# Cross attention on one core: key and value units taken by turns, the keys made two quads in front of their scores

## The chip, the core and the metric

The kernel runs on one core of a Trainium2 chip. Time is the device time of one execution in microseconds (us), less is better. Three runs of the kernel before took 2381.77, 2382.19 and 2385.43 us; their median is 2382.19 us.

The engines are called PE (TensorE, matmuls), DVE (VectorE), ACT (ScalarE), POOL (GpSimd) and SP (SyncE, which issues most transfers). PEld is PE's weight load, which overlaps the matmuls. Each engine takes its instructions in the order in which they are written; between engines, semaphores say who may go on.

## The reference, cut to what matters

A decoder layer of three parts, each with a residual and a layer norm: causal self attention, cross attention to a context of 722 positions, and a gated feed forward. The change is in the cross attention and in the passage from it to the feed forward.

```python
q = (query @ Wq.T + bq).reshape(b, lq, HEADS, HEAD_DIM)
k = (key @ Wk.T + bk).reshape(b, lk, HEADS, HEAD_DIM)
v = (value @ Wv.T + bv).reshape(b, lk, HEADS, HEAD_DIM)
scores = jnp.einsum('bqhd,bkhd->bhqk', q * scale, k)
probs = jax.nn.softmax(scores, axis=-1)
attn = jnp.einsum('bhqk,bkhd->bqhd', probs, v).reshape(b, lq, HIDDEN)
return attn @ Wo.T + bo
```

There are 32 batches of 100 query tokens, 512 features and 16 heads of 32. Key and value both come from the same context, `ctx_1024` (32 x 722 x 512). Everything is fp32; the large products are made of three products of a high and a low part each.

## The kernel before

**Quads, pairs and steps.** The cross attention works in steps. Two steps, a pair, serve one quad: four heads of one batch. A batch has four quads, all batches have 128, so there are 256 steps (`STEPS`). The scores of quad q are written at step 2q; its weighted sum (probabilities times values) is written four steps, two pairs, later (`SUM_AFTER`).

**Units.** The keys of a batch are made in 8 key units: unit u gives one half of the 722 positions (384 or 338 columns, `HALVES`) for one quad, so a quad needs two. The values of a batch are made in 6 value units of 128 positions and 512 columns each; in 7 of 32 batches there are 5, because their last rows share a unit with other batches (tails). Each unit is 12 matmuls of PE (line 69). The tables `KEYS_AHEAD`, `V_STEP` and `FOURTH_V_STEP` give each unit its step: before, the two key units of a quad stand in the pair just in front of the pair of its scores. A pair holds two key units and one or two value units.

**The order on PE.** In a pair: the scores (L2057, 36 matmuls, into the four-bank tile `ps_s`), the units of the pair (`units_of_pair`, sorted: all keys, then all values), and the weighted sum of the quad two pairs back (`weighted_sum`, L2081).

**Two banks.** Units and weighted sums take the two PSUM banks `ps_p` in strict turn. `wait_bank` makes PE wait, before it writes the n-th item, until the (n-2)th has been read out: a key unit by DVE (`k_low`), a value unit by ACT (`v_done`), a weighted sum by DVE (`scaled`).

**ACT.** For a pair: four exponentials (`exps`, L1687; each reads one head of the scores and needs DVE's maxima), the key units' high parts (`take_keys`, L1667), the value units (`take_values`, L1675) and four transfers of the diagonal blocks of the turned probabilities (`move_diagonal`, L1697).

**DVE.** For a pair: the result of a weighted sum out of PSUM (`take_result`, L1847), four maxima (L1820), four block transposes of the exponentials (`turn_blocks`, L1829), the low parts of two key units (`low_keys`, L1872), a reciprocal (L1835) and its transpose (L1840).

**POOL and SP.** POOL splits each batch's context into high and low parts, four pieces, in the pairs that begin at steps 6 and 10 of the batch two before (L1554, L1556), and spreads the inverses. SP issues twelve transfers of turned blocks per quad, the context and the queries.

**The start.** Four steps (from -4) lie ahead of the first scores. DVE takes no key unit before it has read a maximum over all partitions, which POOL makes (L1865).

**The end.** The last pairs are written out by hand: the first five output projections (`project_o`, into `ps_y`), the last two score quads, the last weighted sums, the sum and norm of the first tiles (`second_sum`, `normalise`), the transposes (`transpose_x2`). `TAIL` is the first quad whose weighted sum takes bank 0 whatever its turn. `project_o(0, 0)` waits for the split output weights (`wo_low`, DVE L1973), the split first outputs (`o_low`, DVE L1978 and POOL), all keys and values, and the results of all quads below `TAIL`.

Of the kernel before, what the change touches and what calls it, by code (L numbers as in the profile page):

```python
# [1 line left out]

# [11 lines left out]
KD = D // P  # L14
# [7 lines left out]
QUADS = H // 4  # L22
# [1019 lines left out]
def phase_cross_and_feed_forward(nc, sem, passed, ctxT, cq_d, held, bk, bv, o_d, x1_d, wo, bo, w_gate, w_up, w_down, biggest, out):  # L1042
# [19 lines left out]
    KEYS_AHEAD = 2  # L1062
# [21 lines left out]
    TAIL = MAIN // 2 - 1  # L1084
# [6 lines left out]
    with ExitStack() as ctx:  # L1091
# [159 lines left out]
        units_of_pair = {s: sorted(unit_at.get(s, []) + unit_at.get(s + 1, [])) for s in every_step if s % 2 == 0}  # L1251
# [97 lines left out]
        with nc.Block() as block:  # L1349
# [312 lines left out]
            def _(act):  # L1662
# [41 lines left out]
                def take_units(kind, s):  # L1704
                    for which, b, n in unit_at.get(s, []):
                        if which == kind:
                            (take_keys if kind == "k" else take_values)(b, n)

                def quad_at(s):
                    if s >= 0:  # L1710
                        exps(2 * s)
                    take_units("k", s)
                    if s >= 0:
                        exps(2 * s + 1)
                    take_units("k", s + 1)
                    if s >= 0:
                        exps(2 * s + 2)
                        exps(2 * s + 3)
                    if s > 1:
                        move_diagonal(s // 2 - 1)  # L1720
                    take_units("v", s)
                    take_units("v", s + 1)
# [93 lines left out]
            def _(dve):  # L1816
# [63 lines left out]
                def quad_at(s, first_sum=None):  # L1880
# [4 lines left out]
                    low_keys(s)  # L1885
                    turn_blocks(s, 0)
                    low_keys(s + 1)
                    turn_blocks(s, 1)
                    if s == MAIN:
                        take_result(sum_at[s])  # L1890
                    invert(s // 2)
                    turn_blocks(s + 1, 0)
                    turn_inverses(s // 2)
                    if first_sum is not None:
                        second_sum(0, first_sum)
                    turn_blocks(s + 1, 1)
# [92 lines left out]
                quad_at(MAIN, first_sum=0)  # L1989
# [16 lines left out]
                take_biased(QUADS * B - 2)  # L2006
                normalise("a", 3, x2[:, 3, :])
                low_x2(0, 1)
                low_x2(0, 2)
                second_sum(0, 4)  # L2010
# [9 lines left out]
            def _(pe):  # L2020
                def keys_unit(b, u):
                    m, (first, end) = u // 2, HALVES[u % 2]
                    wait_bank(pe, "k", b, u)
# [4 lines left out]
                def values_unit(b, i):  # L2028
                    rows = P if i < ST - 1 else LAST
                    if i == 0:  # L2030
                        pe.wait_ge(c_low, KD * (b + 1))
# [82 lines left out]
                def feed_forward(w, view):  # L2114
# [53 lines left out]
                    weighted_sum(last - 1)  # L2168
                    transpose_x2(0, 1)
                    project_o(0, 4)  # L2170
                    transpose_x2(0, 2)
# [86 lines left out]
```

## Time and profile before

| what | us |
|---|---|
| median of three runs | 2382.19 |
| the profiled execution, whole | 2380.97 |
| its span (first to last instruction) | 2379.2 |
| first scores of the cross attention | at 506.97 |
| scores of quad 125 (the 126th) | at 1838.84 |
| scores of quad 126 | at 1851.26 |
| first gate matmul of the feed forward | at 1889.89 |

Times of the trace are counted from the span's start. The rows below are of five kinds: windows (busy time of each engine in a stretch), the waits of an engine added up, and the timelines of PE, of ACT, POOL and DVE in one pair, the one whose scores start at 1242.84.

### The profile page before, as it was taken

The page shows a single profiled execution, that of the slowest core. Times are in us where ns is not written, and L with a number is a line of the kernel's source. Part 1 is how long each engine was busy: PE and PEld are TensorE (multiplying, and loading weights), DVE is VectorE, ACT ScalarE, POOL GpSimd, SP SyncE. Part 2 cuts the span into 40 slices and gives each one's busy share as a digit, 9 for nine tenths or more (in the row PEclk, how much of TensorE's full clock was granted, in tenths as well). Part 3 has the DMA queues.
Part 4 walks back from the last instruction along what each step waited for, and adds up shares of the span by engine and source line. Part 5 has one row for each costly group of instructions (what it writes and reads, how often), then busy time and mean ns, then how long its engine had stood idle before and what let it go on. Part 6 is the DMA issues. An engine that isn't in the chain of part 4 may idle for free.

```text
span 2379.2 us, 61357 instructions
## 1 busy us (share of the span) xinstructions
PE 2322.6 (98%) x23178; PEld 2039.2 (86%) x23178; DVE 1642.2 (69%) x2566; ACT 1139.5 (48%) x3066; POOL 1016.0 (43%) x1337
## 2 busy tenths in 40 slices
PE   8999979999999999999999999999999899999999
PEld 7878858978888888888888888888888799998998
DVE  4666788847878788787778787787787734435342
ACT  5878852234555555455554555555555442231321
POOL 4767677334334344334343344343332333333332
PEclk9999989999999999999999999999999999999999
DMA  7444478547777777777777777777777741102010
GB/s 191 130 130 114 121 210 322 208 118 188 196 197 197 199 196 202 196 199 201 194 194 203 191 203 197 195 203 189 197 199 209 214 133 36 50 18 66 8 33 23
DMA packets 256370, 384.77 MB, mean 162 GB/s; under 512 B 118296, under 2 KB 133720, under 8 KB 256088
## 3 DMA queue, kind: packets, MB, share of 16 engines
q1 hardware_dynamic: 231512, 330.66, 49.9%
q10 hardware_dynamic: 24576, 50.36, 7.8%
q8 instruction: 176, 2.88, 0.5%
q14 instruction: 106, 0.87, 0.1%
HBM read 126.33 MB, written 40.60 MB: 70 GB/s over the span
## 4 chain that ended last, share of the span: by engine, by line
PE 76%; DVE 1%; issue 1%; DMA 0%; ACT 0%; POOL 0%; ACTq 0%; POOLq 0%; DVEq 0%
PE D_ps_p L69 43%; PE D_ps_s L2057 7%; PE D_ps_p L2081 6%; PE E_ps_u L69 6%; PE E_ps_g L69 6%; PE E_ps_d L69 5%; PE E_ps_y L69 3%; PE E_ps_t L2110 0%; DVE D_columns L1820 0%; DMA D_pT<-D_turned 0%; DVE D_turned L1829 0%; DVE E_wo_low L1973 0%; ACT D_e L1687 0%; DVE D_keys L1872 0%; ACTq L1697 0%
## 5 line engine op out<-in xcount | busy, mean ns | idle before, releaser
L1687 ACT ACTIVATE D_e<-D_ps_s,D_columns 128x726 f32<-128x726 f32 x512 | 441.4, 868 | 442.3 <-DVE D_columns L1820 442.3
L1820 DVE TENSOR_REDUCE D_columns<-D_ps_s 128x1 f32<-128x726 f32 x512 | 432.3, 907 | 121.6 <-PE D_ps_s L2057 121.6
L1829 DVE STREAM_TRANSPOSE D_turned<-D_e 128x768 f32<-128x768 f32 x512 | 491.2, 960 | 0.0
L69 PE MATMUL D_ps_p<-D_ctx_high,cross_wk_high 128*128 128x384 f32 (+1 forms) x1024 | 345.6, 338 | 0.0
L69 PE MATMUL D_ps_p<-D_ctx_high,cross_wk_low 128*128 128x384 f32 (+1 forms) x1024 | 332.7, 325 | 0.0
L69 PE MATMUL D_ps_p<-D_ctx_low,cross_wk_high 128*128 128x384 f32 (+1 forms) x1024 | 332.3, 325 | 0.0
L69 PE MATMUL D_ps_p<-cross_wv_high,D_ctx_high 128*128 128x512 f32 (+1 forms) x656 | 269.6, 411 | 5.6 <-DVE D_keys L1872 4.1
L1538 POOL COPY D_turned<-D_turned_inv 128x100 f32<-128x100 f32 x128 | 34.8, 272 | 551.2 <-DVE D_turned_inv L1840 551.2
L69 PE MATMUL D_ps_p<-cross_wv_high,D_ctx_low 128*128 128x512 f32 (+1 forms) x656 | 257.3, 392 | 0.0
L69 PE MATMUL D_ps_p<-cross_wv_low,D_ctx_high 128*128 128x512 f32 (+1 forms) x656 | 257.1, 392 | 0.0
L1675 ACT ACTIVATE D_values<-D_ps_p 128x512 f32<-128x512 f32 (+1 forms) x185 | 110.8, 599 | 242.4 <-PE D_ps_p L69 210.9
L1556 POOL TENSOR_TENSOR D_ctx_low<-D_craw,D_ctx_high 128x722 fp32r<-128x722 f32 x124 | 217.1, 1751 | 10.0
L69 PEld LDWEIGHTS D_ps_p<-D_ctx_high,cross_wk_high 128*128 128x128 f32 x1024 | 192.0, 188 | 15.5
L650 ACT ACTIVATE A_e<-A_e,A_neg_max 100x100 f32<-100x100 f32 x512 | 186.4, 367 | 37.1 <-DVE A_neg_max L779 36.3
L1953 DVE SCALAR_TENSOR_TENSOR E_gated<-E_ps_u,E_gated 128x320 f32<-128x320 f32 x120 | 59.0, 491 | 209.6 <-ACT E_gated L1756 209.6
L69 PEld LDWEIGHTS D_ps_p<-D_ctx_low,cross_wk_high 128*128 128x128 f32 x1024 | 192.3, 188 | 0.0
L69 PEld LDWEIGHTS D_ps_p<-D_ctx_high,cross_wk_low 128*128 128x128 f32 x1024 | 192.2, 188 | 0.0
L1599 POOL TENSOR_TENSOR E_hidden_low<-E_gated,E_hidden_high 128x320 fp32r<-128x320 f32 x120 | 105.0, 876 | 182.6 <-ACT E_hidden_high L1749 182.6
L2081 PEld LDWEIGHTS D_ps_p<-D_pT,D_values 128*32 128x32 f32 x5920 | 126.9, 108 | 47.9 <-issue 46.0
L1533 POOL TENSOR_SCALAR D_o<-D_o,D_columns 128x100 f32<-128x100 f32 x125 | 66.9, 535 | 235.8 <-DVE D_o L1847 235.8
L69 PEld LDWEIGHTS D_ps_p<-cross_wv_high,D_ctx_high 128*128 128x128 f32 (+1 forms) x656 | 122.8, 187 | 50.8 <-DVE D_keys L1872 16.8
L2081 PE MATMUL D_ps_p<-D_pT,D_values 128*32 128x100 f32 x5920 | 155.8, 250 | 2.7 <-DVE D_keys L1872 1.7
(271 smaller groups left out, 5594.7 us busy)
## 6 DMA issues: line engine op xcount, KB each, us to landing
D_pT<-D_turned SPq DMA_DIRECT2D x1536, 96.0 KB, 2.5
D_pT<-D_turned ACTq DMA_DIRECT2D x512, 96.0 KB, 2.8
D_craw<-in_ctxT SPq DMA_DIRECT2D x124, 361.0 KB, 3.9
self_v<-wstage SPq DMA_DIRECT2D x25, 256.0 KB, 2.6
A_v<-self_v SPq DMA_DIRECT2D x32, 200.0 KB
self_o<-A_o SPq DMA_DIRECT2D x32, 200.0 KB, 4.0
x<-C_x SPq DMA_DIRECT2D x5, 1280.0 KB, 6.0
cross_q<-C_qo SPq DMA_DIRECT2D x20, 320.0 KB, 4.2
```

The costliest lines, as they stand in the source:

```text
L69: last = pe.matmul(out, lhs(a, k), rhs(b, k), start=(k == 0 and n == 0), stop=(k == chunks - 1 and n == len(terms) - 1))
L650: act.activation(head, head, ACT.Exp, bias=neg_max[:, b % 2, h:h + 1], accum_out=rowsum[:, half, i:i + 1]).then_inc(exp_done, 1)
L1533: pool.tensor_scalar(rows, rows, bv_c[:, m:m + 1], None, ALU.add).then_inc(o_done, 1)
L1556: pool.tensor_tensor(cs[b % 2][1][:, k, 0:S], craw[k % 2][:, :], cs[b % 2][0][:, k, 0:S].bitcast(F32), ALU.subtract).then_inc(c_low, 1)
L1599: pool.tensor_tensor(hs[1][:, c, cols], gated[u % 2][:, :], hs[0][:, c, cols].bitcast(F32), ALU.subtract).then_inc(hl_done, 1)
L1675: act.activation(vs[b % 2][0:rows, i, :], bank("v", b, i)[0:rows, 0:D], ACT.Copy).then_inc(v_done, 1)
L1687: act.activation(e[n // 2 % 2][:, n % 2, 0:PARTS * PART].rearrange("p (a c) -> p a c", a=PARTS), parts_of(n), ACT.Exp, bias=neg_max[:, n % ...
L1820: dve.tensor_reduce(neg_max[:, n % 4:n % 4 + 1], parts_of(n), AX.XY, ALU.max, negate=True)\
L1829: dve.transpose(turned[quad % 2][:, :, 2 * (s % 2) + h, :].rearrange("p j (t r) -> p t j r", r=32), e[s % 2][:, h, :].rearrange("p (t j r) ...
L1953: dve.scalar_tensor_tensor(gated[u % 2][:, :], ps_u[u % 2][:, 0:HALF], FSCALE, gated[u % 2][:, :], ALU.mult, ALU.mult).then_inc(h_done, 1)
L2057: last = pe.matmul(of_head[:, j, a, 0:end - first], qs[q][rows, quad % 2, :, :].rearrange("p a q -> p (a q)"), ks[k][rows, quad % 2, first ...
L2081: last = pe.matmul(out[HD * j:HD * (j + 1), 0:T], values[:, c:c + HD], pT[quad % 2][:, :, j, 32 * i:32 * i + QB], start=(i == 0), stop=(i ...
```

## The change

Six edits, in the code below:

1. `KEYS_AHEAD` goes from 2 to 4: the key units of a quad stand two pairs in front of its scores, no longer one. The last pairs have fewer units, the first ones more.
2. In a pair PE takes key and value units by turns (`by_turns`): key, value, key, and the second value if there is one; then the weighted sum. PE's wait for the split context (`c_low`) goes from the first value unit of a batch to its first key unit, which now stands in the same pair.
3. ACT: first key unit after the first exponential as before; then the three other exponentials, the first value unit, the second key unit, the diagonal transfers, the second value unit.
4. DVE: the low part of the second key unit goes from between the first two transposes to the very end of the pair.
5. `TAIL` is one less. PE's last pair is written by hand: scores, projection 0, weighted sum, projection 1.
6. At the end, the first sum of the second norm stands in front of the transposes of its pair; the weighted sum of quad 126 and its result go behind projection 4.

```diff
-    KEYS_AHEAD = 2
+    KEYS_AHEAD = 4
...
-    TAIL = MAIN // 2 - 1
+    TAIL = MAIN // 2 - 2
...
-        units_of_pair = {s: sorted(unit_at.get(s, []) + unit_at.get(s + 1, [])) for s in every_step if s % 2 == 0}
+        def units_in(s, which):
+
+            return [u for u in unit_at.get(s, []) + unit_at.get(s + 1, []) if u[0] == which]
+
+        def by_turns(s):
+
+            both = itertools.zip_longest(units_in(s, "k"), units_in(s, "v"))
+            return [u for pair in both for u in pair if u is not None]
+
+        units_of_pair = {s: by_turns(s) for s in every_step if s % 2 == 0}
...
                     if s >= 0:
                         exps(2 * s)
-                    take_units("k", s)
+                    take(keys[:1])
                     if s >= 0:
                         exps(2 * s + 1)
-                    take_units("k", s + 1)
-                    if s >= 0:
                         exps(2 * s + 2)
                         exps(2 * s + 3)
+                    take(values[:1])
+                    take(keys[1:])
                     if s > 1:
                         move_diagonal(s // 2 - 1)
-                    take_units("v", s)
-                    take_units("v", s + 1)
+                    take(values[1:])
...
                     low_keys(s)
+                    if s == MAIN:
+                        second_sum(0, 0)
                     turn_blocks(s, 0)
-                    low_keys(s + 1)
                     turn_blocks(s, 1)
                     if s == MAIN:
                         take_result(sum_at[s])
+                    turn_blocks(s + 1, 0)
                     invert(s // 2)
-                    turn_blocks(s + 1, 0)
+                    turn_blocks(s + 1, 1)
                     turn_inverses(s // 2)
-                    if first_sum is not None:
-                        second_sum(0, first_sum)
-                    turn_blocks(s + 1, 1)
+                    low_keys(s + 1)
...
                 second_sum(0, 3)
-                take_biased(QUADS * B - 2)
                 normalise("a", 3, x2[:, 3, :])
                 low_x2(0, 1)
+                second_sum(0, 4)
+                take_biased(QUADS * B - 2)
                 low_x2(0, 2)
-                second_sum(0, 4)
...
                 def keys_unit(b, u):
                     m, (first, end) = u // 2, HALVES[u % 2]
+                    if u == 0:
+                        pe.wait_ge(c_low, KD * (b + 1))
                     wait_bank(pe, "k", b, u)
...
-                    if i == 0:
-                        pe.wait_ge(c_low, KD * (b + 1))
...
                     project_o(0, 3)
-                    weighted_sum(last - 1)
                     transpose_x2(0, 1)
                     project_o(0, 4)
+                    weighted_sum(last - 1)
...
-                for s in range(FIRST, MAIN + 1):
-                    if 0 <= s < STEPS and s % 2 == 0:
+                for s in range(FIRST, MAIN, 2):
+                    if s >= 0:
                         scores(s // 2)
...
+                scores(last - 1)
                 project_o(0, 0)
+                weighted_sum(last - 3)
                 project_o(0, 1)
```

**PE, one pair with a single value unit in the middle of the cross attention.** Each unit is shown by its first matmul (11 more follow). `cross_wk` marks a key unit, `cross_wv` a value unit, `D_ps_p0` and `D_ps_p1` are the two banks, `D_ps_s` the scores, the row with `D_pT` the weighted sum. Before:

```order
7007 L2057 MATMUL D_ps_s<-D_keys_7891,D_queries_low_7895 128x238 x4
7008 L69 MATMUL D_ps_p1<-D_ctx1_high_7882,cross_wk_high 128x384
...
7020 L69 MATMUL D_ps_p0<-D_ctx1_high_7882,cross_wk_high 128x338
...
7032 L69 MATMUL D_ps_p1<-cross_wv_high,D_ctx1_high_7882 128x512
...
7044 L2081 MATMUL D_ps_p0<-D_pT1_7903,D_values0_7896 32x100 x24
```

Of the change:

```order
7031 L2067 MATMUL D_ps_s<-D_keys_7891,D_queries_low_7895 128x238 x4
7032 L70 MATMUL D_ps_p1<-D_ctx1_high_7882,cross_wk_high 128x384
...
7044 L70 MATMUL D_ps_p0<-cross_wv_high,D_ctx1_high_7882 128x512
...
7056 L70 MATMUL D_ps_p1<-D_ctx1_high_7882,cross_wk_high 128x338
...
7068 L2091 MATMUL D_ps_p0<-D_pT1_7903,D_values0_7896 32x100 x24
```

The value unit now stands between the two key units. The bank of the first key unit is asked for again by the second key unit and not by the value unit; the weighted sum asks for the bank of the value unit and not for that of the second key unit.

**ACT, one pair with a single value unit.** `D_e` rows are exponentials, `D_keys` and `D_values` rows read a unit out. Before:

```order
896 L1687 ACTIVATE D_e0_7897,D_columns_7906<-D_ps_s,D_columns_7906 128x726
897 L1667 ACTIVATE D_keys_7891<-D_ps_p0,D_columns_7906 128x384
898 L1687 ACTIVATE D_e0_7897,D_columns_7906<-D_ps_s,D_columns_7906 128x726
899 L1667 ACTIVATE D_keys_7891<-D_ps_p1,D_columns_7906 128x338
900 L1687 ACTIVATE D_e1_7898,D_columns_7906<-D_ps_s,D_columns_7906 128x726 x2
901 L1697 DMA D_pT0_7902<-D_turned0_7899 32x768 x4
902 L1675 ACTIVATE D_values1_7901<-D_ps_p0 128x512
```

Of the change:

```order
898 L1698 ACTIVATE D_e0_7897,D_columns_7906<-D_ps_s,D_columns_7906 128x726
899 L1678 ACTIVATE D_keys_7891<-D_ps_p0,D_columns_7906 128x384
900 L1698 ACTIVATE D_e0_7897,D_columns_7906<-D_ps_s,D_columns_7906 128x726
901 L1698 ACTIVATE D_e1_7898,D_columns_7906<-D_ps_s,D_columns_7906 128x726 x2
902 L1686 ACTIVATE D_values1_7901<-D_ps_p1 128x512
903 L1678 ACTIVATE D_keys_7891<-D_ps_p0,D_columns_7906 128x338
904 L1708 DMA D_pT0_7902<-D_turned0_7899 32x768 x4
```

The value unit goes in front of the second key unit and of the transfers, and stays behind all four exponentials.

**DVE, one pair in the middle, of the change.** Before, the row with 128x338 stood between the two transposes of `D_e0`.

```order
1538 L1857 TENSOR_TENSOR D_o1_7905<-D_ps_p1,D_pT1_7903 128x100
1539 L1830 TENSOR_REDUCE D_columns_7906<-D_ps_s 128x1 x4
1540 L1882 SCALAR_TENSOR_TENSOR D_keys_7891<-D_ps_p0,D_columns_7906,D_keys_7891 128x384
1541 L1839 STREAM_TRANSPOSE D_turned0_7899<-D_e0_7897 128x6x4x32 x2
1542 L1839 STREAM_TRANSPOSE D_turned0_7899<-D_e1_7898 128x6x4x32
1543 L1845 RECIPROCAL D_columns_7906<-D_columns_7906 128x4
1544 L1839 STREAM_TRANSPOSE D_turned0_7899<-D_e1_7898 128x6x4x32
1545 L1850 STREAM_TRANSPOSE D_turned_inv_7893<-D_columns_7906 128x128
1546 L1882 SCALAR_TENSOR_TENSOR D_keys_7891<-D_ps_p0,D_columns_7906,D_keys_7891 128x338
```

The low part of the second key unit is the last row of the pair now.

## Rows read from the trace of the kernel before

**Rows 1.** Windows: bounds, length, busy (instructions) of PE, PEld, DVE, ACT, POOL, clock, DMA.

```profile
499.70:507.00 7.30, 7.29 (x28) 5.59 (x28) 0.43 (x1) 0.60 (x1) 0.92 (x2) 0.77 0.00 0
506.97:1838.84 1331.87, 1331.87 (x15565) 1151.43 (x15564) 1056.00 (x1622) 686.74 (x1456) 524.13 (x801) 1.00 0.74 197
...
1860.91:1889.89 28.98, 22.97 (x208) 17.40 (x209) 22.52 (x41) 8.64 (x14) 5.80 (x9) 0.88 0.94 280
```

**Rows 2.** Waits of PE's weight loads, 500 to 1870: us, times, longest.

```profile
PEld D_ps_p L69 <- DVE D_keys L1872: 12.4, 74, 0.4
```

**Rows 3.** Timeline of PE in one pair: start, us, engine, line, operation.

```profile
1242.84 0.50 PE L2057 MATMUL D_ps_s<-D_keys,D_queries_high 32*128 32x242 f32 x8
...
1244.09 0.44 PE L69 MATMUL D_ps_p<-D_ctx_high,cross_wk_high 128*128 128x384 f32 x1
...
1246.28 0.31 PE L69 MATMUL D_ps_p<-D_ctx_high,cross_wk_high 128*128 128x338 f32 x1
...
1247.81 0.31 PE L69 MATMUL D_ps_p<-D_ctx_low,cross_wk_high 128*128 128x338 f32 x1
1247.97 0.32 PE L69 MATMUL D_ps_p<-D_ctx_high,cross_wk_low 128*128 128x338 f32 x1
1248.17 0.50 PE L69 MATMUL D_ps_p<-cross_wv_high,D_ctx_high 128*128 128x512 f32 x1
1248.51 0.39 PE L69 MATMUL D_ps_p<-cross_wv_low,D_ctx_high 128*128 128x512 f32 x1
...
1251.12 1.26 PE L2081 MATMUL D_ps_p<-D_pT,D_values 128*32 128x100 f32 x48
1252.30 0.50 PE L2057 MATMUL D_ps_s<-D_keys,D_queries_high 32*128 32x242 f32 x8
```

**Rows 4.** Timeline of PE at the start, from a value unit into a key unit.

```profile
491.31 0.39 PE L69 MATMUL D_ps_p<-cross_wv_high,D_ctx_low 128*128 128x512 f32 x1
491.54 0.33 PE L69 MATMUL D_ps_p<-D_ctx_high,cross_wk_high 128*128 128x384 f32 x1
```

**Rows 5.** Timeline of ACT in the same pair.

```profile
1245.98 0.87 ACT L1687 ACTIVATE D_e<-D_ps_s,D_columns 128x726 f32<-128x726 f32 x1 [3.62 <-DVE D_columns L1820]
...
1246.84 0.57 ACT L1667 ACTIVATE D_keys<-D_ps_p,D_columns 128x384 fp32r<-128x384 f32 x1
1247.30 0.87 ACT L1687 ACTIVATE D_e<-D_ps_s,D_columns 128x726 f32<-128x726 f32 x1
...
1251.22 0.60 ACT L1675 ACTIVATE D_values<-D_ps_p 128x512 f32<-128x512 f32 x1 [0.67 <-PE D_ps_p L69]
```

**Rows 6.** Timelines of DVE and POOL in the same pair.

```profile
1244.21 3.38 DVE L1820 TENSOR_REDUCE D_columns<-D_ps_s 128x1 f32<-128x726 f32 x4 [0.98 <-PE D_ps_s L2057]
1247.50 0.61 DVE L1872 SCALAR_TENSOR_TENSOR D_keys<-D_ps_p,D_columns,D_keys 128x384 fp32r<-128x384 f32 x1
1248.03 0.97 DVE L1829 STREAM_TRANSPOSE D_turned<-D_e 128x768 f32<-128x768 f32 x1
1248.92 0.55 DVE L1872 SCALAR_TENSOR_TENSOR D_keys<-D_ps_p,D_columns,D_keys 128x338 fp32r<-128x338 f32 x1
...
1252.62 0.22 DVE L1847 TENSOR_TENSOR D_o<-D_ps_p,D_pT 128x100 f32<-128x100 f32 x1
...
1247.93 1.75 POOL L1556 TENSOR_TENSOR D_ctx_low<-D_craw,D_ctx_high 128x722 fp32r<-128x722 f32 x1
```

**Rows 7.** Timelines of DVE and PE around the stall at the start.

```profile
499.04 1.08 DVE L1872 SCALAR_TENSOR_TENSOR D_keys<-D_ps_p,D_columns,D_keys 128x384 fp32r<-128x384 f32 x2
...
499.71 0.55 PE L69 MATMUL D_ps_p<-cross_wv_high,D_ctx_high 128*128 128x512 f32 x1 [4.06 <-DVE D_keys L1872]
```

**Rows 8.** Timelines of DVE and PE in the last pairs.

```profile
1848.71 3.60 DVE L1973 TENSOR_TENSOR E_wo_low<-E_wo_raw,E_wo_high 128x512 fp32r<-128x512 f32 x2
1852.23 2.18 DVE L1978 TENSOR_TENSOR E_acts_low<-E_acts_raw,E_acts_high 128x640 fp32r<-128x640 f32 x1
...
1858.54 1.24 PE L2081 MATMUL D_ps_p<-D_pT,D_values 128*32 128x100 f32 x48 [1.73 <-DVE D_keys L1872]
```

More of the change, by code:

```diff
@@ L1 @@
 from contextlib import ExitStack
+import itertools
 import math
@@ L1703, in _, with take @@
                 act.wait_ge(b_loaded, 32)
[L1704 to L1707, printed above, removed]
+                def take(units):
+                    for kind, b, n in units:
+                        (take_keys if kind == "k" else take_values)(b, n)
                 def quad_at(s):
+                    keys, values = units_in(s, "k"), units_in(s, "v")
                     if s >= 0:
                         exps(2 * s)
-                    take_units("k", s)
+                    take(keys[:1])
                     if s >= 0:
                         exps(2 * s + 1)
-                    take_units("k", s + 1)
-                    if s >= 0:
                         exps(2 * s + 2)
                         exps(2 * s + 3)
+                    take(values[:1])
+                    take(keys[1:])
                     if s > 1:
                         move_diagonal(s // 2 - 1)
-                    take_units("v", s)
-                    take_units("v", s + 1)
+                    take(values[1:])
                 def high_o(g):
@@ L1878, in maxima, with quad_at @@
                     maximum(2 * s + 1)
-                def quad_at(s, first_sum=None):
+                def quad_at(s):
                     if s - 2 in sum_at:
@@ L1988, in _ @@
                 last_first_low()
-                quad_at(MAIN, first_sum=0)
+                quad_at(MAIN)
                 normalise("a", 0, x2[:, 0, :])
```

## The prediction

> **What bounds the kernel now.** I read the windows first, then the waits, then one pair of the cross attention on every engine. From the first scores to those of quad 125, 1331.87 of the 2379 us of the span, PE is busy all the time at full clock; DVE is busy 79% and ACT 52% of it [rows 1]. So PE sets the pace and only what PE itself loses counts. Nearly nothing shows as idle, since matmuls overlap; the loss has to be read as the distance between starts. Inside a key unit of 338 columns matmuls follow at 0.153 to 0.16 us, and a value unit's at 0.23 (its last one to the next unit, too) [rows 3, 4]. From the last key matmul to the first value matmul it is 0.20, and from that to the second 0.34 [rows 3]. The sum of both excesses, 0.05 and 0.11, is 0.16 us per pair. Its cause is in the waits: PE's weight load there waits for DVE's `D_keys`, 12.4 us in 74 times, 0.17 each [rows 2]. The value unit takes the bank of the first key unit, whose low part DVE ends only at 1248.11, 0.06 before the value unit starts [rows 3, 6]: DVE must first make four maxima of the scores written just before.
>
> **The pair, part by part.** I count from the start of the scores, 1242.84. Before: first key unit +1.25, second +3.44, value unit +5.33, weighted sum +8.28, next scores +9.46 [rows 3]. There are 125 pairs from quad 0 to quad 125, of which 70 hold one value unit and 55 two (from the step tables).
>
> By turns, the order is key, value, key, (value), sum. Who waits for whom now:
> - Value unit at +3.44. It wants the bank of the sum or value before it, which is read early; the wait is gone. It takes 12 x 0.228 = 2.73, to +6.17.
> - Second key unit at +6.17. It wants the bank of the first, whose low part ends at +5.27 [rows 6]. ACT and DVE treat the first key unit as before. Slack 0.9. It takes 12 x 0.153 = 1.84, to +8.01.
> - Second value unit, or the weighted sum, at +8.01. It wants the first value unit's bank, read by ACT behind all four exponentials. ACT: exponential at +3.14, key at +4.00, exponential at +4.46 [rows 5]; from one exponential to what follows it is 0.86, so the others start at +5.32 and +6.18 (the maxima are there at +4.66 [rows 6]), and the value is read from +7.04 to +7.64, its 0.60 as now [rows 5]. PE asks for it with the weight load, 0.15 ahead of +8.01. Slack 0.2 in front of a value unit, near 0.45 in front of the sum, whose weights don't load ahead. This is the tightest place of the change.
> - The sum behind a second value unit wants the second key unit's bank, at +10.7. DVE's low part of it now ends the pair. DVE as a whole does the same work: the result of the sum came at +9.78 [rows 6], so the low part ends by then. The same holds for a pair with one value unit, in which the next first key unit wants that bank, at +10.5. Slack 0.7.
> - The next pair's scores need keys that were made a pair earlier, and their four exponentials, ended by +7.1. No wait. DVE ends at +10.0 and the next maxima can start at 9.30 + 1.37 = +10.67: DVE still idles 0.6 per pair and doesn't become the bound.
> - ACT's diagonal transfers move behind the second key unit's readout, by 2 us; they are for a sum a whole pair later (+17). Queued behind them on ACT is only the second value unit, which PE ends at about +10.9. SP's transfers start when the last transpose is done, which is earlier than now, as the low part has left the space ahead of it.
> - PE's wait for the split context moves from the value unit to the first key unit of the same pair. POOL ends the last piece at 1249.68 [rows 6], and the key unit that would need it starts at 1252.30 + 1.25 = 1253.55. Nothing waits. Moving a wait that is satisfied costs nothing.
>
> So a pair loses its 0.16: 125 x 0.16 = 20.0 us by the one pair, 125 x 0.17 = 21.3 by the waits. I take **-21**. Bounds: what the four edges do when all waits are satisfied isn't in the trace for key into value; value into key is, at 0.23 with nothing added [rows 4], and that is the nearest row. At worst that spacing is intrinsic, and the gain 0; at best the pairs with longer waits (the longest are 0.4 [rows 2]) bring it to -24.
>
> The Trainium skill would have the spacing smaller (TensorE: Matmul & The Clock Gate, Back-to-back issue gap: columns over 2.4 GHz plus 2.5 ns), that is 0.216 us for 512 columns and 0.143 for 338. By that estimate PE would be back at the value's bank at about +7.75 and not +8.01, near enough to wait for ACT in the pairs with two value units. The trace has 0.23 and 0.153 [rows 3, 4], and the measurement decides.
>
> **The start.** PE has two banks. Before, value, key, key went ahead of the stall; the fourth item waited until 499.71 for DVE, which takes keys only from 499.04 [rows 7]. Now the third item (the second key unit) wants the first key unit's bank and stalls to the same 499.7, with 1.84 us of work less behind it. After the stall come key 1.84, key 2.08 (12 x 0.174 from [rows 3]), value, key, value: 11.3 us, to 511.0 at full clock. The clock row gives 0.77 of full clock for the 7.3 us after the stall [rows 1], a loss of 7.3 x 0.23 = 1.7 us; with the same loss the first scores start at 512.7, against 506.97. That is **+5.8**, of which 3.9 are the two key units that move here from the end. PE now idles 6 us instead of 4, so the low stretch could start sooner and cost less, or last longer: +4.1 with no loss, +7.5 with twice the loss.
>
> An idle array is throttled and regains its clock after work, says the Trainium skill (TensorE: Matmul & The Clock Gate, What's actually happening); the 0.77 behind a stall of 4.06 us agrees.
>
> **The end.** From the scores of quad 125 (1838.84) to the first gate matmul (1889.89) are 51.05 us. Two key units, 3.9 us, and PE's wait of 1.73 for their low part [rows 8] leave. They don't all become gain, as DVE holds the end: its 3.60 for the output weights and 2.18 for the first outputs stand ahead of the result that projection 0 waits for [rows 8]. By the same timetable DVE ends the keys of that pair at about +10.2 from 1838.84, the two splits at +15.9, the result at +16.1: projection 0 starts near 1855 instead of 1860.91. From there on DVE's maxima, transposes and sums set the pace; it was busy 22.5 of the next 29 us [rows 1], and no longer hides PE's work as well: six us ahead shrink to some four at the gate, with a clock that still falls in PE's gaps (0.88 [rows 1]). The weighted sum behind projection 4 covers the transfers it waits for. I take **-4**. Bounds: -1.2 (DVE sheds only two low parts, 0.61 + 0.55) and -6. Behind the gate nothing changes; an earlier gate moves all of the feed forward.
>
> **The sum.** -21 + 5.8 - 4 = -19.2. The profiled execution took 2380.97; 2380.97 - 19.2 = 2361.8. The median of the three runs stands 1.2 above it, so I forecast **2363.0**.
>
> **Rivals.**
> - *Half of it.* ACT's value readout is late in the pairs with two value units, or the longer turn order lets other waits of 0.1 appear. For: 0.2 us of slack from a timetable of 0.01 us rows. Against: ACT is idle half the time and each step of it is in a row. Gain some 10 less: 2373.
> - *The spacing from key to value is the array's own*, and the wait beside it covers nothing. For: it was always seen together with a wait. Against: [rows 4]. Then +5.8 - 4: 2384.
> - *Slower: ACT's four exponentials hold the value's bank.* Each microsecond by which the value is read later than my +7.64 costs the same on PE, beyond 0.2 in 55 pairs and 0.45 in 70. It breaks even with all else where 125y - 42.5 = 19.2, y = 0.5 us, a readout that ends at +8.14. With y = 0.6 the time is 2382 + 32.5 - 19.2 = 2395. For: before, this readout was never waited for by a unit in the same pair, and a single exponential is 0.86. Against: no order of ACT's instructions but the written one is possible, and nothing in it waits later than the maxima. Had the skill's spacing been true, the break-even would be nearer by 0.26.
> - The change does what it says: the built order of PE, ACT and DVE shows it.
>
> **How the numbers follow.** Forecast 0.79, half 0.10, none 0.05, slower 0.06. The range 2354 to 2374 takes the forecast with its bounds (-24 + 4.1 - 6 at best, -17 + 7.5 - 1.2 at worst) and most of the half. A measurement of this kernel can tell 0.2%, 4.8 us, from no change. Faster by more: 0.89; within: 0.05; slower: 0.06.
>
> **What would show it.** Right: pairs of 9.30 us where they were 9.46; 0.23 between the last value and the next key matmul; 0.17 or less from the last key to the first value matmul; no wait of PE for `D_keys` in the middle; ACT's value readout ended by +7.7; first scores near 512.7; some 47 us from quad 125 to the gate. Wrong: a wait of PE for ACT's `D_values` ahead of second value units or sums, a wait for `D_turned`'s transfers, DVE without idle time ahead of its maxima, or a first score after 515.

## The result and the profile after

The change made the kernel no faster, and if anything 3.8 us slower. Its median is 2386.98 us (2380.64 to 2392.29, 20 runs), against 2383.18 (2377.09 to 2386.64, 20 runs) of the kernel before. The ratio is 1.0016, with a 95% interval of 1.0008 to 1.0023, which leaves out 1. The forecast was 2363.0 with a range up to 2374, so it was wrong by 24 us.

The traces are compared in three stages, cut at starts on PE: the first unit of the cross attention, the first scores, the scores of quad 125, the first gate matmul.

| stage, us | before | after | forecast |
|---|---|---|---|
| start: first unit to first scores | 18.30 | 24.91 | 24.1 |
| steady: to the scores of quad 125 | 1331.87 | 1333.93 | 1310.9 |
| end: to the first gate matmul | 51.05 | 52.32 | 47.0 |

The profiled execution of the change took 2390.93 us, 4 above its median, and that of before 2380.97, 2 below. The stages add up to the 10 us between these two; by the medians it is 3.8. Ahead of the first unit and behind the gate the two differ by 1.5 us in opposite directions.

The windows of the changed kernel (start, steady, end) answer to [rows 1]; columns as there:

```profile
487.15:512.06 24.91, 19.01 (x84) 16.87 (x84) 2.67 (x7) 3.44 (x6) 9.83 (x18) 0.86 0.25 78
...
512.06:1845.99 1333.93, 1319.83 (x15565) 1161.93 (x15565) 1044.42 (x1622) 672.06 (x1454) 519.16 (x795) 1.00 0.76 196
1845.99:1898.31 52.32, 38.64 (x429) 30.13 (x425) 45.42 (x73) 21.34 (x40) 18.26 (x24) 0.93 0.84 234
```

PE, which was busy for all 1331.87 us of the steady part [rows 1], now stands for 1333.93 - 1319.83 = 14.1 us of it. Nearly all of this, 13.9 us, it waits for DVE's `D_keys`: 8.6 ahead of weighted sums and 5.3 ahead of units. Its busy time is 12 us less: the saving is there, and new waits eat it. The waits view of the whole kernel names them (us, times, longest); the first two stood at nothing and at 8.6 before:

```profile
DVE D_turned L1839 <- DMA D_pT<-D_turned: 37.0, 30, 3.4
POOL D_ctx_high L1565 <- DMA D_craw<-in_ctxT: 36.9, 20, 2.9
...
PE D_ps_p L2091 <- DVE D_keys L1882: 9.5, 13, 2.1
```

PE waits for nothing of POOL's in this part, so POOL's longer wait for the context is not what costs the time.

The wait that the change was to remove [rows 2] is gone from the middle of the pair. DVE instead waits for the transfers of `pT`, which the forecast had put aside as a whole pair early. One such wait, on ACT, DVE and PE, from the scores at 1250.13 on:

```profile
1258.41 0.54 ACT L1678 ACTIVATE D_keys<-D_ps_p,D_columns 128x338 fp32r<-128x338 f32 x1 [0.69 <-PE D_ps_p L70]
1258.49 3.73 ACTq L1708 DMA_DIRECT2D D_pT<-D_turned  x4
```

```profile
1264.15 0.61 DVE L1882 SCALAR_TENSOR_TENSOR D_keys<-D_ps_p,D_columns,D_keys 128x384 fp32r<-128x384 f32 x1
1267.66 2.70 DVE L1839 STREAM_TRANSPOSE D_turned<-D_e 128x768 f32<-128x768 f32 x3 [2.91 <-DMA D_pT<-D_turned]
...
1271.40 0.53 DVE L1882 SCALAR_TENSOR_TENSOR D_keys<-D_ps_p,D_columns,D_keys 128x338 fp32r<-128x338 f32 x1
```

```profile
1271.98 0.44 PE L70 MATMUL D_ps_p<-D_ctx_high,cross_wk_high 128*128 128x384 f32 x1 [1.85 <-DVE D_keys L1882]
```

ACT issues the four diagonal transfers when the second key unit's readout begins, 8.36 us behind the scores; before it was 5.83. They belong to the quad of the pair before. `turn_blocks` of the pair that follows writes the buffer that they read, waits until they have landed (`moved_sem(quad - 2)`), and so stands 2.91 us. The low half of the second key unit, which the change has put behind all four transposes, comes at 1271.40, and PE waits 1.85 us for its bank. The transfers run beside SP's loads of context and tails. Of the stretch 1258 to 1264, and then of the whole page, the issues view says (KB each, median us to landing):

```profile
D_craw<-in_ctxT SPq DMA_DIRECT2D x2, 361.0 KB, 5.2
D_pT<-D_turned ACTq DMA_DIRECT2D x4, 96.0 KB, 5.4
```

```profile
D_pT<-D_turned ACTq DMA_DIRECT2D x512, 96.0 KB, 2.9
```

Pairs without such a wait did get shorter. With one value unit the median is 9.34 us (9.49 before), with two 12.09 (12.18). But 16 of the 55 pairs with two value units are over 12.4 us, and hold 14.9 us more than their median.

### The profile page after: what moved, and what is told of

Its sections match the earlier page's. It is cut to its first block, busy times and chain, and to the rows that moved or that the text cites. A ratio compares the mean times of both kernels' runs of the same rounds, so it can differ in the third digit from the quotient of the medians.

```text
span 2389.1 us, 61358 instructions
## 1 busy us (share of the span) xinstructions
PE 2318.2 (97%) x23178; PEld 2056.9 (86%) x23178; DVE 1631.7 (68%) x2566; ACT 1125.4 (47%) x3066; POOL 1015.8 (43%) x1337
## 4 chain that ended last, share of the span: by engine, by line
PE 64%; DVE 6%; issue 4%; DMA 3%; ACTq 1%; ACT 1%; POOL 0%; DVEq 0%; POOLq 0%
PE D_ps_p L70 33%; PE E_ps_g L70 6%; PE E_ps_u L70 6%; PE D_ps_s L2067 6%; PE D_ps_p L2091 5%; PE E_ps_d L70 5%; DVE D_turned L1839 3%; DMA D_pT<-D_turned 3%; PE E_ps_y L70 3%; DVE D_columns L1830 2%; ACTq L1708 1%; ACT D_e L1698 0%; DVE D_keys L1882 0%; PE E_ps_t L2120 0%; DVE D_turned_inv L1850 0%
## 5 line engine op out<-in xcount | busy, mean ns | idle before, releaser
L1839 DVE STREAM_TRANSPOSE D_turned<-D_e 128x768 f32<-128x768 f32 x512 | 462.9, 947 | 51.7 <-DMA D_pT<-D_turned 37.0
L70 PE MATMUL D_ps_p<-cross_wv_high,D_ctx_high 128*128 128x512 f32 (+1 forms) x656 | 255.7, 390 | 0.1
L70 PEld LDWEIGHTS D_ps_p<-D_ctx_high,cross_wk_high 128*128 128x128 f32 x1024 | 193.2, 189 | 33.9 <-DVE D_keys L1882 12.5
L1678 ACT ACTIVATE D_keys<-D_ps_p,D_columns 128x384 fp32r<-128x384 f32 (+1 forms) x256 | 142.8, 558 | 116.1 <-PE D_ps_p L70 98.1
L2067 PE MATMUL D_ps_s<-D_keys,D_queries_high 32*128 32x242 f32 (+1 forms) x3072 | 155.0, 294 | 0.0
```

Source lines behind the costliest of these rows:

```text
L70: last = pe.matmul(out, lhs(a, k), rhs(b, k), start=(k == 0 and n == 0), stop=(k == chunks - 1 and n == len(terms) - 1))
L1678: act.activation(ks[0][:, m % 2, first:end], bank("k", b, u)[:, 0:end - first], ACT.Identity, bias=bk_c[:, m:m + 1]).then_inc(k_high, 1)
L1839: dve.transpose(turned[quad % 2][:, :, 2 * (s % 2) + h, :].rearrange("p j (t r) -> p t j r", r=32), e[s % 2][:, h, :].rearrange("p (t j r) ...
L2067: last = pe.matmul(of_head[:, j, a, 0:end - first], qs[q][rows, quad % 2, :, :].rearrange("p a q -> p (a q)"), ks[k][rows, quad % 2, first ...
```

## The experiments

Stages in us as above, each from one profiled execution; median and ratio are of 4 to 10 executions, and the ratio is to the kernel before, run on the same chip. The change itself lies 3.8 us above the kernel before by the medians.

| kernel | start | steady | end | median | ratio, 95% |
|---|---|---|---|---|---|
| e1_before_key2 | 24.80 | 1319.38 | 51.43 | 2375.57 | 0.9971 (0.9961 to 0.998) |
| e2_after_exps | 24.61 | 1352.65 | 49.43 | 2405.96 | 1.0091 (1.0074 to 1.0107) |
| e3_before_late | 18.21 | 1332.56 | 53.95 | 2383.23 | 0.9999 (0.9989 to 1.0009) |
| e4_start_v_first | 23.45 | 1353.95 | 48.04 | 2405.51 | 1.0094 (1.0077 to 1.0111) |
| e5_before_late | 19.24 | 1337.04 | 53.92 | 2393.16 | 1.0050 (1.0033 to 1.0067) |
| e6_e1_v_first | 22.22 | 1319.63 | 50.32 | 2372.78 | 0.9960 (0.9946 to 0.9974) |
| e7_light_loads | 24.30 | 1318.24 | 53.21 | 2374.92 | 0.9972 (0.9961 to 0.9984) |
| e8_e1_flag_later | 17.61 | 1319.67 | 50.46 | 2372.40 | 0.9953 (0.9935 to 0.997) |
| e9_before_flag | 17.81 | 1332.28 | 50.76 | 2382.70 | 0.9999 (0.9988 to 1.001) |
| e10_rstd_first | 18.16 | 1320.52 | 46.76 | 2365.60 | 0.9926 (0.9898 to 0.9954) |
| e11_split | 17.76 | 1317.83 | 48.04 | 2364.97 | 0.9923 (0.9901 to 0.9946) |
| e12_together | 17.87 | 1318.11 | 45.93 | 2363.03 | 0.9919 (0.9906 to 0.9933) |

### e1 and e2: ACT's transfers earlier in the changed kernel

```diff
                     take(values[:1])
-                    take(keys[1:])
                     if s > 1:
                         move_diagonal(s // 2 - 1)
+                    take(keys[1:])
                     take(values[1:])
```

> The changed kernel with one step of ACT moved: the four diagonal transfers of a quad are issued ahead of the second key unit's readout instead of behind it, so some 0.8 to 1.3 us earlier in the pair (at about +7 us after the scores instead of +8.4). Theory A, the long pairs come from late transfers (turn waits for transfer, 37.0 us in the profile of the change): that wait falls, but not to nothing, since +7 is still 1.2 us behind the +5.8 of the kernel before: 10 to 25 us are left, and scores(0) to scores(125) goes from 1333.9 to 1322 to 1330. Theory B, the long pairs come from DVE's own order (the second key's low half behind all four turns) and the transfers only go with them: the stretch stays within 1332 to 1336.

The transfers now start at +6.50. The wait has vanished, and the steady part is 14.5 us shorter than in the change, better than theory A had it; theory B falls. The profile of the change had lain 4 us above its median: by the medians, against the kernel before on each chip, e1 is 8.0 us faster and the change 3.8 slower, 11.8 us apart. In the changed kernel's own page the transposes' group ended with `51.7 <-DMA D_pT<-D_turned 37.0`. The other 14 us of these 51.7 are ten waits that the waits view puts down to ACT's exponentials. The first exponential, which is all that the first transpose needs of ACT, had ended 1.4 to 3.5 us before those waits did, and in nine of the ten a transfer of `D_turned` landed at most 0.1 us ahead of their end. So they are most likely the same wait. In e1:

```profile
L1839 DVE STREAM_TRANSPOSE D_turned<-D_e 128x768 f32<-128x768 f32 x512 | 462.6, 948 | 1.1 <-ACT D_e L1698 1.1
```

e2 puts them ahead of `take(values[:1])` as well.

> The changed kernel with the four diagonal transfers issued right behind the four exponentials, ahead of both readouts: the place in time they have in the kernel before, about +5.8 us after the scores. Theory A: the turn's wait for the transfer goes from 37.0 to under 5 us, no pair over 12.3 us is left but for a few, and scores(0) to scores(125) is 1318 to 1322, so 12 to 16 us less than in the changed kernel; the whole is 2370 to 2376, ratio to the kernel before 0.994 to 0.997. Theory B (DVE's order): the transfer wait may go, but the stretch stays at 1330 or more and the ratio at 1.000 to 1.002. Theory C, the loads of context and tails on SP take the DMA engines whenever the transfers come: the wait stays above 20 us.

The wait is gone here too (0.5 us are left), yet the steady part is 33 us longer than in e1. None of the theories had this. ACT in one pair, scores at 1297.05, and what PE's weight loads wait for ACT's value readouts (us, times, longest):

```profile
1302.59 0.62 ACTq L1708 DMA_DIRECT2D D_pT<-D_turned  x1
...
1303.24 1.25 ACTq L1708 DMA_DIRECT2D D_pT<-D_turned  x2
...
1304.55 0.60 ACT L1686 ACTIVATE D_values<-D_ps_p 128x512 f32<-128x512 f32 x1 [0.39 <-issue]
```

```profile
PEld D_ps_p L70 <- ACT D_values L1686: 20.5, 56, 1.9
```

An issue costs ACT's queue 0.6 us. The four end at +7.44 and hold the value readout back from +6.97 to +7.50, which used up the 0.2 to 0.45 us of slack that the forecast gave this readout. That is the typical pair; in single pairs PE waits up to 2.1 us for this readout. This is the forecast's slow rival in another form. The Trainium skill (DMA: Bandwidth & Descriptors, Issuing engines are not separate DMA queues) says that the sequencer's time to start a DMA is usually small beside the DMA itself. Here it is, with 0.6 of 2.8 us, and decides all the same, by what it stands in front of.

### e3 and e5: the transfers late in the kernel before

```diff
-                    if s > 1:
-                        move_diagonal(s // 2 - 1)
                     take_units("v", s)
+                    if s > 1:
+                        move_diagonal(s // 2 - 1)
                     take_units("v", s + 1)
```

> The kernel BEFORE with one step of ACT moved: the four diagonal transfers behind the value unit's readout, so at about +8.4 us after the scores instead of +5.8, which is where the change puts them; nothing else is touched. Theory A: the kernel before now gets the same waits (turn for transfer 15 to 40 us, none before) and loses 5 to 20 us, ratio 1.002 to 1.008. Theory B (DVE's order of the change makes the long pairs): no wait of that kind over 3 us and ratio 0.999 to 1.001.

No wait and no loss, as theory B had it, but the edit didn't test what it should: in most pairs with one value unit that unit belongs to `s + 1`, so the transfers moved (to +8.46) only in pairs with two, where 12.18 us of pair leave them time. e5 moves them behind the first value readout of every pair.

> The kernel BEFORE with ACT's four diagonal transfers behind the pair's first value readout in every pair. The third run had moved them only in pairs with two value units (from +5.83 to +8.46 us after the scores), and a turn that follows such a pair has 12.18 + 5.18 us for them, enough. Now they start at +8.4 in pairs with one value unit too, and the turn of the next pair comes 9.5 + 5.2 = 14.7 behind the same scores. Theory A (a late start, in a pair of one value unit with loads behind it, is what makes the long pairs): turn waits for transfers appear in 20 to 30 pairs, 20 to 40 us in sum, and scores(0) to scores(125) is 1340 to 1350 instead of 1331.9; ratio 1.003 to 1.007. Theory B (DVE's order of the change is needed for it): no such wait, 1331 to 1333, ratio 1.000.

```profile
DVE D_turned L1832 <- DMA D_pT<-D_turned: 37.6, 38, 2.7
```

Late transfers alone make the same waits in the kernel before: 37.6 us against 37.0 in the change, or 41.2 against 51.1 with those put down to ACT. In its profile the steady part is 5.2 us longer (1337.04, under theory A's 1340 to 1350). By the medians e5 is 10.9 us slower than the kernel before, nearly the 11.8 that lie between the change and e1. So whether the wait costs less here is open. The low half of the second key unit stands behind the first transpose here, not the fourth; what this order adds wasn't tried by itself.

### e7: the change with light loads

From context 3 on each context load brings 64 of 722 columns; the rest of the context is left out, and old values are computed with.

```diff
-                    sp.dma_start(craw[k % 2][:, :], c_rows[b, :, k, :]).then_inc(c_loaded[k % 2], 16)
+                    part = slice(0, S if b < 3 else 64)
+                    sp.dma_start(craw[k % 2][:, part], c_rows[b, :, k, part]).then_inc(c_loaded[k % 2], 16)
```

> The changed kernel, with ACT's transfers late as the change has them, but from context 3 on each of SP's context loads brings only 64 of 722 columns (32 KB instead of 361 KB): left out is the rest of the context, whose old values are computed with. All else as in the change. Theory A1 (late and beside the loads: the transfers take 5.4 us from issue to landing beside them, 2.8 otherwise): the turn's wait for transfers falls from 37.0 to under 8 us and scores(0) to scores(125) from 1333.9 to 1319 to 1323. Theory A2 (lateness alone, with ACT's issues at 0.6 to 1 us each; the bytes don't matter): 25 us of wait or more stay, and 1330 or more.

```profile
DVE D_turned L1840 <- DMA D_pT<-D_turned: 7.6, 12, 1.8
```

With ACT's order as in the change, 7.6 of the 37.0 us are left and the steady part is 1318.24. So the long pairs need both: transfers that start late, and big loads beside them. The same section of the Trainium skill has it that DMAs started by different engines run on the same 16 DMA engines and interleave. The runs fit that: ACT's transfers take 5.4 us beside SP's loads and 2.9 as the median of the whole profile.

### e4, e6, e8, e9: the start

e4 is e2 with value, key, key in the pairs ahead of the first scores, e6 the same on e1.

> As the second kernel of this set, and in the pairs ahead of the first scores the value unit goes first (value, key, key) on PE and ACT. At the start PE stands for the second load of context with only two units behind it in the changed kernel, key and value. By the sum, nothing of it is gained: five further units are needed whatever their order, first unit to first scores 24.9 us within 0.5. Rival: a unit more ahead of the stall shortens it: 22 to 23.5 us, and the whole is 1.5 to 3 us under the second kernel of this set.

> The changed kernel with the transfers ahead of the second key readout (as the first run), and value, key, key ahead of the first scores. By the fourth run the start is 1.3 us shorter (23.45 instead of 24.8 from the first unit to the first scores); the steady part is 1319 to 1320 as in the first run. Together 2374.3, ratio 0.9965 within 0.001. If turns and start touch each other otherwise, the first scores come later than +24.0.

One more unit ahead of the stall shortened the start by 1.2 us on e2 and 2.6 on e1, as e4's rival had it, though e4's whole is only 0.5 us under e2's. e4's text took the stall for a wait for context. It isn't one, and e8 takes it away:

```diff
-                dve.wait_ge(all_max, 2)
-                dve.tensor_scalar(inexact[:, :], biggest_all[:, :], EXACT, None, ALU.is_gt).then_inc(flagged, 1)
...
                 for s in range(FIRST, 0):
                     low_keys(s)
+                dve.wait_ge(all_max, 2)
+                dve.tensor_scalar(inexact[:, :], biggest_all[:, :], EXACT, None, ALU.is_gt).then_inc(flagged, 1)
```

> As the first run, and at the start DVE computes the flag inexact (for which it waits 10.00 us for POOL's all-reduce, with the first low keys queued behind it) behind the low keys of the pairs ahead of the first scores. Theory S (PE's stall at the start is this wait): the stall of 5.7 to 5.9 us behind the second unit goes, no stretch at half clock follows it, and first unit to first scores goes from 24.8 to 17 to 19 us; it can't be under 17.5 since POOL's first low queries end at +17.4. The whole is 2368 to 2370, ratio 0.993 to 0.995. Rival: the keys then wait for something else at the start (ACT's first readout came at +4.1, behind POOL's zeroing), and only 2 to 4 us are gained.

In the changed kernel DVE and PE had stood like this:

```profile
497.42 0.15 DVE L1875 TENSOR_SCALAR inexact<-biggest_all 128x1 int32<-128x1 f32 x1 [10.00 <-POOL biggest_all L1635]
```

```profile
498.16 0.65 PE L70 MATMUL D_ps_p<-D_ctx_high,cross_wk_high 128*128 128x338 f32 x1 [5.90 <-DVE D_keys L1882]
```

A wait for a flag that is read only at the feed forward held the first low keys, and they held PE. e8's start is 17.61 us (its whole, 2372.40, is above the 2368 to 2370 expected), and the window has the full granted clock where the change had 0.86:

```profile
493.40:511.01 17.61, 16.76 (x84) 14.58 (x85) 2.66 (x7) 3.86 (x7) 4.38 (x13) 1.00 0.21 66
```

> The kernel BEFORE with DVE's flag (and its wait for POOL's all-reduce) moved behind the low keys ahead of the first scores; nothing else. In the previous set this took 7.2 us from the changed start (24.8 to 17.6). Theory: it is the same wait that stops PE before (4.06 us ahead of the fourth unit), so that stall goes, but the first scores can't start before POOL's first low queries, +17.4 behind the first unit: 18.3 goes to 17.3 to 17.8, the whole gains 0.5 to 1.5 us, ratio 0.9993 to 1.0000. Then nearly all of the 6.5 us that the change loses at the start is this wait, and with it moved the change starts level. Rival: the queries come earlier when DVE is free, and the start falls to 14 to 16.

In e9 the kernel before has no stall either, but gains nothing, since PE arrives early and then stands 5.34 us ahead of the first scores; POOL's first low queries end only then. So the two key units that the change moves to the front cost nothing once the flag is out of the way.

### e10, e11, e12: the end, a split, and all together

```diff
+                rstd_of("a", 0)
                 spread_inverses(last - 1)
-                rstd_of("a", 0)
```

> The fourth kernel of the previous set (transfers ahead of the second key readout, flag later), and at the end POOL computes the first row's reciprocal deviation ahead of the spread of quad 126's inverses. In that kernel projection 0 starts at +16.6 behind quad 125's scores, 5.4 earlier than in the kernel before, and the first normalise at +28.04, no earlier than the 27.87 there. Theory T1 (the gain at the end is lost as POOL keeps that value back until DVE's inverses are turned): the 0.93 us of DVE's wait goes and the gate comes 0.7 to 1.2 us sooner, +49.3 to 49.8 instead of 50.46. T2 (DVE is full there and only its order counts): nothing, 50.2 to 50.8, since the following sums wait for the transposes either way.

The end fell by 3.7 us, more than either theory said. Part of it is the clock: projection 0 ran at a granted clock of 0.62 in e8 and at 1.00 in e10. The edit's own part is read between e11 and e12, which differ by it alone, and in which projection 0 is as short as in e10. DVE's first normalise in e11, then in e12:

```profile
1847.13 1.49 DVE L1922 TENSOR_SCALAR E_x<-E_r_a,E_mv_a,E_rstd_a 128x512 f32<-128x512 f32 x1 [0.93 <-POOL E_rstd_a L1596]
```

```profile
1849.09 0.50 DVE L1922 TENSOR_SCALAR E_x<-E_r_a,E_mv_a,E_rstd_a 128x512 f32<-128x512 f32 x1
```

0.93 us of waiting and 0.99 of the operation itself (below) are gone, and the end is 2.11 shorter. That DVE's wait goes, as T1 says, is shown. The size, twice T1's, rests on one profile of each, and the intervals of e11 and e12 overlap.

e11 is e8 with `move_diagonal(s // 2 - 1, (0, 2))` ahead of the first value readout and `(1, 3)` behind it.

> Again the fourth kernel of the previous set, with ACT's four transfers split: two behind the exponentials, ahead of the first value readout, two behind it. All four ahead of that readout cost 33 us (the second run: 4 issues of 0.62 us from +5.00 hold the readout back from +6.97 to +7.50, and PE's second key unit waits for that bank). Theory I (it is the time the issues take on ACT's queue): two end at +6.3, ahead of +6.97, so the value readout isn't late, pairs stay at 9.34 to 9.36 and 12.08 to 12.11, scores(0) to scores(125) 1317 to 1320. Theory II (transfers in flight at that time disturb PE or ACT, whatever their issues): half of the 33 us comes back, 1330 to 1340.

Theory I holds: with only two issues ahead, the readout isn't late, and the steady part is 1317.83.

> The changed kernel with the four edits that helped, together: two of ACT's transfers ahead of the first value readout and two behind it, DVE's flag behind the low keys of the start, and the first reciprocal deviation ahead of the spread on POOL at the end. Each has been measured: start 17.6 to 18.2 (change 24.9), scores(0) to scores(125) 1317.8 (change 1333.9), end 46.8 to 48.0 (change 52.3). If they add up, start + steady + end is 1382.5 to 1384 against 1401.2 of the kernel before, 18 us less: 2364 with the end at 48, 2361 to 2363 with the end at 46.5 or less; ratio 0.991 to 0.9925, and below both runs of the previous set that have only two of the three. If the POOL edit and the split ask for the same time at the end, it is no faster than 2365.

The stages hold all three gains at once: 1381.91 us in sum against 1401.22, 19.3 less, and the median is 20.8 us under that of the kernel before. By their intervals e10, e11 and e12 can't be told apart. Windows of e12, start, steady and end:

```profile
488.54:506.41 17.87, 16.74 (x85) 14.56 (x85) 2.67 (x7) 4.04 (x7) 4.37 (x13) 1.00 0.20 65
506.41:1824.52 1318.11, 1318.11 (x15566) 1160.78 (x15566) 1042.04 (x1623) 672.00 (x1455) 524.19 (x801) 1.00 0.74 199
1824.52:1870.45 45.93, 36.42 (x429) 29.25 (x425) 43.80 (x73) 20.74 (x39) 18.27 (x23) 0.96 0.84 242
```

## Why the prediction was wrong

**The step that failed** is "ACT's diagonal transfers move behind the second key unit's readout, by 2 us; they are for a sum a whole pair later (+17)". The 2 us were right (5.83 to 8.36; 2.5). The reader was not: the first to ask isn't the sum at +17 but `turn_blocks` at the next pair's +5.18, that is +14.5, which overwrites their source. The last of the four is issued by about +11 (+12.1 in the pair shown), and takes 5.4 us to land beside the loads, so it lands behind +14.5; in the pair shown it let the turn go at +17.5. e1 (earlier: wait gone, -14.5), e7 (light loads: -15.7) and e5 (late in the kernel before: the wait appears) show it. The forecast's list of what would be wrong did hold "a wait for `D_turned`'s transfers", yet no rival had a price for it.

**The pair: right in kind, too large.** By e1, where next to nothing waits, the steady part gains 12.5 us, and by e11 14.0, not 21. The forecast counted 0.17 for each of 125 pairs, but 0.17 is the mean of the 74 waits in [rows 2], which hold 12.4 us in all. The gain that came is near that sum; that it is the same time wasn't shown. In e1, pairs with one value unit went from 9.48 to 9.34 on average (-0.14, forecast -0.16), those with two from 12.16 to 12.11 (-0.05, forecast the same 0.16 to 0.17). The edges in a pair of the changed kernel:

```profile
1262.75 0.33 PE L70 MATMUL D_ps_p<-D_ctx_high,cross_wk_low 128*128 128x384 f32 x1
1262.92 0.39 PE L70 MATMUL D_ps_p<-cross_wv_high,D_ctx_high 128*128 128x512 f32 x1
...
1267.39 0.32 PE L70 MATMUL D_ps_p<-D_ctx_high,cross_wk_low 128*128 128x338 f32 x1
1267.64 1.08 PE L2091 MATMUL D_ps_p<-D_pT,D_values 128*32 128x100 f32 x40
```

From key to value it is 0.17, as forecast, so the spacing rival falls. From the last key matmul into the sum it is 0.25, against 0.155 inside the unit. The forecast had +8.01 for that start; it came at +8.16, and the next scores at +9.34, not +9.30. With two value units, the one ahead of the sum takes 2.85 us where it took 2.81, and each other unit 0.02 or 0.03 more than twelve of its inner distances. The forecast had set all edges but the two with a wait at nothing. The -17 at the near end of its range has no term behind it either.

**ACT's value readout: right.** It starts at +6.97 and ends at +7.6. Next to nothing waits for it in the change. e2 shows how near it is: 0.53 us later costs 33 us, where the rival's formula (125y - 42.5) gives 24.

**The start: right.** +6.6 against +5.8 and within the bounds. The stretch from the first unit to the fifth shows a granted clock of 0.80. That the stall is the flag's wait, and could be moved, played no part in the forecast, though the description of the kernel names the wait (L1865) and [rows 7] show DVE taking keys only from 499.04; e8 and e9 show it.

**The end: wrong in size.** Projection 0 was to start 16.2 us behind the scores of quad 125 and did at 16.5 in e1, against 22.1 before. In the change it came at 18.35. That is the step that failed once more: the first transpose of quad 125 starts at +7.79 there and at +5.97 in e1. The last transfer of quad 123, issued at +0.84 beside two loads of 256 KB, took 6.8 us to land, until +7.69. The profile names ACT's exponential, but that had ended at +4.7:

```profile
1853.78 2.70 DVE L1839 STREAM_TRANSPOSE D_turned<-D_e 128x768 f32<-128x768 f32 x3 [1.90 <-ACT D_e L1698]
```

```profile
D_pT<-D_turned ACTq DMA_DIRECT2D x1, 96.0 KB, 6.8
```

Of the 5.5 us nearly nothing reaches the gate in e1 and e8 (51.43 and 50.46). DVE paces the rest, as the forecast said, and waits for POOL. Part of it is the clock: from the first to the last of its twelve starts projection 0 takes 4.2 us in e1 and e8, with a granted clock of 0.62 in e8, and 2.6 before. In e4 and e11 it takes 2.6 too and starts at 15.75, and the end is 48.04 in both, 3.0 us shorter than before, though of the end they touch only where ACT issues its transfers. The 1.6 of the clock and the 0.9 of the earlier start would be all that e8's end has above theirs (an estimate from these rows). With the edit of e12 it is 45.93, so the -4 was there to be had. The same end differs by 3 us between profiles of like kernels (51.05, 53.95), so differences of 1 us in it are not told apart.

**The sum again:** -12.5 clean, +14.5 waits, +6.6 start and +1.3 end make the +9.9 between the profiles. By the medians the whole is +3.8.

## What to carry to other kernels

When an instruction moves later, list everyone who waits for its semaphore, the writer of its source buffer as well as the reader of its result, and price the tightest. A transfer's time is from its issue to its landing beside what else is queued there, not the median of the page. An issue is work too: four of them ahead of a readout with 0.2 to 0.45 us of slack cost more than the wait they were to cure. A wait for a value that is needed much later belongs behind the work that others wait for.

## What the runs showed of the hardware

Beside two loads of 361 KB and four smaller loads the transfers of 96 KB took 5.4 us to land instead of 2.9. Issuing one takes ACT's queue 0.6 us, and took 0.9 on average in the pair shown, beside the loads (3.73 us for four). A normalise of DVE took 1.49 us beside an addition of POOL, and 0.50 without one; of the 50 in e12 one stands beside such an addition and takes 1.50, the others 0.50 to 0.55. In e11, where it started at 1847.13, POOL did:

```profile
1847.08 1.26 POOL L1591 TENSOR_TENSOR E_y<-E_y,E_bo_b 128x512 f32<-128x512 f32 x1
```

DVE's addition at 1849.73 in e12 (L1929), which reads one of its inputs from PSUM, took 0.69 us beside the same addition of POOL, no more than in e11 without it. DVE's split of two blocks of the output weights in the change took 1.28 us in one place of the last pairs, where POOL shows nothing, and 3.99 in the next, beside 5.45 us of POOL's split of the first outputs. That is read from the traces; no run took POOL's work away. Last, PE's distance at the switch from one kind of unit to another is 0.02 to 0.10 us above that inside a unit, even where no wait is shown.
